# Two graph attention layers on 128 graphs: one rotation of four PSUM banks, both layer 1 sums in the odd slot, and the upper parts of k and lk ahead of the layer 1 norm rows on ScalarE

## The chip, the core and the metric

The kernel runs on one core of a Trainium2 chip. The metric is the device time of one execution in microseconds; below 2867.19 us (the median of three runs, 2866.46 to 2871.12) stands for the kernel before.

## What is computed

The input x holds 128 graphs of 128 nodes with 512 features each, adj their 128 x 128 boolean adjacency. Two layers follow one another, each with a residual sum:

```
h = max(layernorm(x), 0)
# layer 0, 8 heads of 64:
m = h @ map_w.T + map_b;  q, k = m @ q_w.T + q_b, m @ k_w.T + k_b
cos_adj = cosine(m_head_i, m_head_j) > 0.1          (masked)
p = softmax(where(mask, -1e10, q k^T / 8)) * keep
A = cos_adj * p;  x = x + relu((A @ (h @ gcn_map_w.T + b)) @ gcn_W.T / (rowsum(A) + 1))
# layer 1, 4 heads of 64:
h = max(layernorm(x), 0)
x = x + softmax(where(adj, (h Wq)(h Wk)^T / 8, -max)) @ (h Wv) @ Wo + bo
```

## The kernel before

All matrices are float32 in the reference and are held here as an upper and a lower float16 part. A product of two such takes three matmul passes (upper by upper, upper by lower, lower by upper). To split a tile, ScalarE copies it to float16 (a function named ..._upper), and GpSimd or VectorE subtracts that from the float32 tile (..._lower). Small per-node tiles are then turned by transposing DMAs that SP issues.

The work is a software pipeline written out by hand. A slot belongs to one graph, and in slot n each stage serves the graph of its own distance: projections of m are two graphs ahead, q and k one ahead, layer 0 scores serve graph n, layer 1 runs 3 to 5 behind. Even and odd slots have different work, since the projections treat two graphs at once (256 columns): the even slot has m, v and lv, the odd one q, k, lq and lk. Each of the five engines has its own function slot(s) that lists its stages in order, separately for even and odd, and over_slots writes all slots of all engines out one after another. There is no planner: an engine does its list in order, and semaphores hold it wherever a stage needs something of another engine. A stage at the head of an engine's list therefore holds back everything behind it in that list.

TensorE's list in the even slot: layer 0 scores, cosines, layer 1 scores (l1_scores), m in two halves, the weighted sums, output (wo), va, lv, vb, the layer 1 sums. In the odd slot: scores, cosines, q in two halves, weighted sums, layer 1 sums, norms, the first half of k, lq, the spreading of the inverse norms (bc0, bc1), the second half of k, output, lk.

A unit is what one of these stages writes into one PSUM bank of 512 floats. Before, there are two pairs of banks: proj_ps (13 units in a pair of slots) and mix_ps (7 units). Within each pair the banks alternate in the order of PROJ_UNITS and MIX_UNITS; start_proj and start_mix make TensorE wait until the unit two places back in the same pair has been read (proj_out, mix_out). proj_full and mix_full tell the readers that a unit is done.

The stages that matter at the boundary from odd to even slot, on ScalarE (L848 on): directions_upper twice, h1_rows (waits for ln1_step, that is GpSimd's norm_l1), qk_upper for the second half of k, h1_upper, lqk_upper for lk. On VectorE: k_lower (L966) for that half, result (L1084), lqk_lower (L991) for lk, and then the next slot's scores_mask. On GpSimd in the odd slot: ..., q_lower, e_lower (L588), directions_lower twice (L650), norm_l1 (L659 to L664), o1_lower (L577). TensorE's scores at the head of the even slot (L1313, s_ps) wait for k_lo, q_lo and x1_done; l1_scores waits for lk's lower part. In the trace both halves of q and k are called qk_sb (float32) and qk_hl (parts), and all of matmul helper row_pairs stands at L1313, features at L1295, rows at L1303.

Of the kernel before, what the change touches and what calls it, by code (L numbers as in the profile page):

```python
# [39 lines left out]
P = 128  # L40
# [40 lines left out]
class Slot:  # L81
# [20 lines left out]
    def _unit(self, units, name, back):  # L102
        def index(t):
            n = 0
            for u in range(FIRST_SLOT, t):
                n += sum(0 <= u + ahead < self.graphs for _, ahead in units[u % 2])
            for what, ahead in units[t % 2]:
                if what == name:
                    return n
                n += 0 <= t + ahead < self.graphs  # L110
            raise KeyError(name)

        at = Slot(self.n - back, self.i, self.graphs)
        return Unit(index(at.n) % 2, at.at(lambda t: index(t) // 2), at.at(lambda t: index(t) + 1))

    def proj(self, name, back=0):
        return self._unit(PROJ_UNITS, name, back)

    def mix(self, name, back=0):
        return self._unit(MIX_UNITS, name, back)  # L120

# [33 lines left out]
def build(nc, x, adj, map_w, map_b, q_w, q_b, k_w, k_b, gcn_map_w, gcn_map_b, gcn_W, Wq, Wk, Wv, Wo, bo, out):  # L155
# [13 lines left out]
    with ExitStack() as ctx:  # L169
# [115 lines left out]
        proj_ps = ctx.enter_context(nc.psum_tensor("proj_ps", [P, 2, 4 * P], F32))  # L285
        mix_ps = ctx.enter_context(nc.psum_tensor("mix_ps", [P, 2, 4 * P], F32))
# [32 lines left out]
        proj_full = sem("proj_full")  # L319
        proj_out = [sem(f"proj_out{i}") for i in range(2)]  # L320
        mix_full = sem("mix_full")
        mix_out = [sem(f"mix_out{i}") for i in range(2)]
# [70 lines left out]
        def prep_bank(u):  # L393
            return (proj_ps, mix_ps)[u % 4 // 2][:, u % 2]
# [18 lines left out]
        def _(sp):  # L413
# [17 lines left out]
            def turn_o1(s):  # L431
                if s.has(-5):
                    sp.wait_ge(o1_lo, s.at(lambda t: t - 5 + 1))
                    settle(sp, settled_sp, s.i)
                    if s.has(-6):
                        sp.wait_ge(proj_full, s.proj("wo", back=1).full)
# [4 lines left out]
            def turn_h1(s):  # L441
                if s.has(-2):
# [3 lines left out]
                    if s.has(-4 - back):  # L446
                        sp.wait_ge(proj_full, s.proj("lv", back=back).full)
# [4 lines left out]
            def turn_p1(s, behind):  # L452
                if s.has(-behind):
                    sp.wait_ge(p1_lo, s.at(lambda t: t - behind + 1))
                    settle(sp, settled_sp, s.i)
                    if s.has(-behind - 2):
                        sp.wait_ge(mix_full, s.mix("o1", back=behind - 2).full)
# [27 lines left out]
            def store(s):  # L485
                if s.has(-5):
                    u = s.proj("wo")
                    sp.wait_ge(proj_out[u.bank], u.before + 1)
                    settle(sp, settled_sp, s.i)
                    sp.dma_start(out[s.graph(-5)], ybuf[:, s.n % 2, :]).then_inc(y_out, 16)  # L490

            def turn_x(s):
                for a in range(2):
                    if s.has(3 + a):
                        sp.wait_ge(h_lo, s.at(lambda t: t + 3 + a + 1))
                        settle(sp, settled_sp, s.i)
                        if s.has(-1):
                            sp.wait_ge(proj_full, s.proj("k23", back=2).full)
# [40 lines left out]
        def _(pool):  # L539
# [72 lines left out]
            def keep_and_block(s):  # L612
# [7 lines left out]
                if s.has(0):  # L620
                    if s.has(-4):
                        u = s.mix("s1b", back=1) if s.odd else s.mix("s1a")
                        pool.wait_ge(mix_out[u.bank], u.before + 1)
# [9 lines left out]
            def inverse_norms(s):  # L633
                if s.has(1):
                    u = s.mix("norm")
                    pool.wait_ge(mix_out[u.bank], u.before + 1)
                    nc.gpsimd.tensor_tensor(inv_norm[:, :], sq_sum[:, :], minus_half[:, :], ALU.pow).then_inc(inv_norm_done, 1)  # L637
                    if s.has(-1):
                        pool.wait_ge(mix_full, s.mix("bc1", back=2).full)
# [85 lines left out]
        def _(act):  # L725
# [35 lines left out]
            def v_upper(s, name, ahead):  # L761
                if s.has(ahead):
                    u = s.proj(name)
                    act.wait_ge(proj_out[u.bank], u.before + 1)
# [5 lines left out]
            def lv_upper(s):  # L770
                if s.has(-4):
                    u = s.proj("lv")
                    act.wait_ge(proj_full, u.full)
                    if s.has(-5):
                        act.wait_ge(mix_full, s.mix("o1", back=1).full)
                    r = (s.n - 4) % 4
                    nc.scalar.activation(lv_sb[:, 0, r:r + 2, :, 0:DH],
                                         proj_ps[:, u.bank, :].rearrange("p (a h d) -> p a h d", a=2, h=H1),
# [29 lines left out]
            def o1_upper(s, behind):  # L808
                if s.has(-behind):
                    u = s.mix("o1", back=behind - 4)  # L810
                    act.wait_ge(mix_out[u.bank], u.before + 1)
# [3 lines left out]
            def qk_upper(s, name, src, dst, half, done):  # L815
                if s.has(1):
                    u = s.proj(f"{name}{2 * half}{2 * half + 1}")
                    act.wait_ge(proj_out[u.bank], u.before + 1)
# [4 lines left out]
            def squares(s):  # L823
                if s.has(2):
                    u = s.proj("m23")
                    act.wait_ge(proj_out[u.bank], u.before + 1)
                    if s.has(0):
                        act.wait_ge(mix_full, s.mix("norm", back=1).full)
                    nc.scalar.activation(sq_t[:, :, :], m_sb[:, :, :], ACT.Square).then_inc(squared, 1)

            def directions_upper(s, g):
                if s.has(1):
                    u = s.mix(f"bc{g}")
                    act.wait_ge(mix_out[u.bank], u.before + 1)
# [5 lines left out]
            def lqk_upper(s, name, dst, k):  # L840
                if s.has(-3):
                    u = s.proj(name)
                    act.wait_ge(proj_full, u.full)
                    if s.has(-5):
                        act.wait_ge(mix_full, s.mix("s1b", back=1).full)
                    nc.scalar.activation(dst[:, 0].rearrange("p c n -> p (c n)"), proj_ps[:, u.bank, :], ACT.Copy,
                                         scale=unscale[:, k:k + 1]).then_inc(lqk_hi, 1)

            def slot(s):
                if s.odd:  # L850
# [45 lines left out]
        def _(dve):  # L896
# [21 lines left out]
            def l1_mask(s, behind):  # L918
                if s.has(-behind):
                    b = (s.n - behind) % 2  # L920
                    u = s.mix("s1a" if behind == 4 else "s1b")
# [552 lines left out]
```

## Time and profile before

| what | value |
|---|---|
| median of three runs | 2867.19 us |
| the profiled execution | 2866.04 us, its span 2864.2 us |
| TensorE busy | 2635.6 us, 92% |
| VectorE, GpSimd, ScalarE busy | 70%, 70%, 59% |
| TensorE's mean granted clock | 0.972 |
| mean busy share of the DMA engines | 53.5% |

The span runs from the first to the last instruction of the execution that the profiler recorded; the rest of its time lies around it. Busy time of an engine is the union of its instructions' times. Matmuls overlap one another, so a busy TensorE need not be at its peak. "Idle before" an instruction is the time in which its engine did nothing just ahead of it, with the operation that ended the wait behind an arrow.

### The profile page before, as it was taken

The numbers are of one execution on the slowest core, as the hardware profiler recorded it, in microseconds if no ns is written. First come the engines' busy times: TensorE is split into PE (matmuls) and PEld (weight loads), VectorE is DVE, ScalarE is ACT, GpSimd is POOL, SyncE is SP. The second block draws the span as 40 slices with busy tenths as digits, with TensorE's granted clock in tenths as the row PEclk, the third lists the DMA queues.
The fourth block names the chain that finished last, engine by engine and source line by source line (L and its number), as shares of the span: only waits on it lengthen the run. The fifth ranks groups of instructions, "written<-read, shape, count | busy, mean of one in ns | idle before, by whom it ended". The sixth has DMA issues, their size and how long they took to land.

```text
span 2864.2 us, 78990 instructions
## 1 busy us (share of the span) xinstructions
PE 2635.6 (92%) x30809; PEld 2103.3 (73%) x30809; DVE 2011.8 (70%) x3457; ACT 1684.7 (59%) x4501; POOL 1993.1 (70%) x2332
## 2 busy tenths in 40 slices
PE   5789999999999999999999999999999999999985
PEld 3567777777777777777777777777777777777763
DVE  4367777777777777777777777777777777777763
ACT  1256666665666655666665566566556656656653
POOL 0377677677677677777877777787777778767762
PEclk7899999999999999999999999999999999999997
DMA  3145555655555555655655565565566555555543
GB/s 100 35 87 107 102 107 114 104 105 111 103 104 112 111 105 108 118 101 108 114 109 109 105 119 103 105 114 110 101 115 117 102 107 114 110 96 114 113 87 71
DMA packets 829123, 299.08 MB, mean 104 GB/s; under 512 B 772560, under 2 KB 778192, under 8 KB 828752
## 3 DMA queue, kind: packets, MB, share of 16 engines
q1 hardware_dynamic: 828752, 294.04, 53.5%
q8 instruction: 245, 4.01, 0.6%
q14 instruction: 126, 1.03, 0.1%
HBM read 75.80 MB, written 33.55 MB: 38 GB/s over the span
## 4 chain that ended last, share of the span: by engine, by line
PE 54%; POOL 24%; issue 8%; DVE 7%; ACT 3%; DMA 2%; SPq 1%; DVEq 0%; ACTq 0%; POOLq 0%
PE proj_ps L1295 23%; PE proj_ps L1303 18%; POOL inv_norm L637 6%; POOL e_ec L588 4%; POOL dir_hl L650 4%; PE s_ps L1313 4%; PE c_ps L1313 3%; POOL qk_hl L609 2%; POOL inv_rows L643 2%; DVE qk_hl L966 2%; PE mix_ps L1313 2%; ACT qk_hl L821 2%; DMA o_t<-o_hl 2%; PE s_ps L1354 1%; POOL rstd L662 1%
## 5 line engine op out<-in xcount | busy, mean ns | idle before, releaser
L732 ACT ACTIVATE e_ec<-e_ec,neg_mx 128x128 f32<-128x128 f32 x1024 | 396.0, 388 | 4.3
L966 DVE TENSOR_TENSOR qk_hl<-qk_sb,qk_hl 128x512 f16<-128x512 f32 x128 | 125.2, 978 | 355.0 <-ACT qk_hl L821 354.6
L583 POOL TENSOR_TENSOR p_hl<-p_sb,p_hl 128x512 f16<-128x512 f32 x128 | 148.3, 1159 | 314.8 <-ACT p_hl L753 314.8
L1295 PE MATMUL proj_ps<-h_t,w_m_hi 128*128 128x256 f16 x2048 | 350.7, 278 | 9.4 <-DMA h_t<-h_hl 9.4
L1295 PE MATMUL proj_ps<-h_t,w_k_hi 128*128 128x256 f16 x2048 | 344.6, 274 | 0.0
L1295 PE MATMUL proj_ps<-h_t,w_q_hi 128*128 128x256 f16 x2048 | 339.5, 273 | 0.0
L1303 PE MATMUL proj_ps<-w_v_hi,h_t 128*128 128x512 f16 x1024 | 325.4, 379 | 0.0
L588 POOL TENSOR_TENSOR e_ec<-e_ec 128x1024 f16<-128x1024 f32 x128 | 287.2, 2244 | 17.1 <-ACT e_ec L759 17.1
L1295 PE MATMUL proj_ps<-h_t,w_m_lo 128*128 128x256 f16 x1024 | 283.9, 277 | 0.0
L1295 PE MATMUL proj_ps<-h_t,w_k_lo 128*128 128x256 f16 x1024 | 280.1, 274 | 0.0
L1295 PE MATMUL proj_ps<-h_t,w_q_lo 128*128 128x256 f16 x1024 | 279.1, 273 | 0.0
L786 ACT ACTIVATE h_sb<-x,shift,rstd 128x512 f32<-128x512 f32 x128 | 103.4, 808 | 231.5 <-POOL shift L664 231.5
L1313 PE MATMUL s_ps<-qk_hl 64*128 64x128 f16 x3072 | 112.6, 222 | 130.3 <-DVE qk_hl L966 130.3
L1295 PEld LDWEIGHTS proj_ps<-h_t,w_m_hi 128*128 128x128 f16 x2048 | 198.8, 100 | 42.7 <-issue 12.2
L571 POOL TENSOR_TENSOR h_hl<-h_sb,h_hl 128x512 f16<-128x512 f32 x128 | 153.9, 1203 | 104.6 <-ACT h_hl L794 104.6
L1295 PEld LDWEIGHTS proj_ps<-h_t,w_q_hi 128*128 128x128 f16 x2048 | 195.2, 98 | 28.5
L1295 PEld LDWEIGHTS proj_ps<-h_t,w_k_hi 128*128 128x128 f16 x2048 | 196.4, 98 | 21.9
L637 POOL TENSOR_TENSOR inv_norm<-sq_sum,minus_half 128x16 f32<-128x16 f32 x64 | 186.5, 2913 | 26.3 <-DVE sq_sum L1025 26.3
L1313 PEld LDWEIGHTS s_ps<-qk_hl 64*128 64x128 f16 x3072 | 89.7, 97 | 152.2 <-DVE qk_hl L966 148.1
L943 DVE SCALAR_TENSOR_TENSOR qk_sb<-proj_ps,unscale,bias_q 128x512 f32<-128x512 f32 x128 | 96.2, 751 | 144.1 <-PE proj_ps L1295 143.9
L1303 PEld LDWEIGHTS proj_ps<-w_v_hi,h_t 128*128 128x128 f16 x1024 | 100.1, 98 | 128.9 <-DVE m_sb L943 20.2
L1303 PE MATMUL proj_ps<-w_v_lo,h_t 128*128 128x512 f16 x512 | 194.0, 379 | 0.0
(205 smaller groups left out, 7866.9 us busy)
## 6 DMA issues: line engine op xcount, KB each, us to landing
xa<-in_x_dram SPq DMA_DIRECT2D x128, 256.0 KB, 3.5
xres<-in_x_dram SPq DMA_DIRECT2D x128, 256.0 KB, 2.8
out_dram<-ybuf SPq DMA_DIRECT2D x128, 256.0 KB, 2.5
h_t<-h_hl SPq DMA_TRANSPOSE x256, 3.2
ec_t<-e_ec SPq DMA_TRANSPOSE x256, 3.2
adj_in<-in_adj_dram SPq DMA_DIRECT2D x128, 16.0 KB, 2.1
p_t<-p_hl SPq DMA_TRANSPOSE x128, 3.3
o_t<-o_hl SPq DMA_TRANSPOSE x128, 3.8
```

Source lines behind the costliest of these rows:

```text
L571: nc.gpsimd.tensor_tensor(h1_hl[:, a, 1, :], h1_sb[:, a, :], h1_hl[:, a, 0, :], ALU.subtract).then_inc(h1_lo, 1)
L583: nc.gpsimd.tensor_tensor(p1_hl[:, b, 1], p1_sb[:, b], p1_hl[:, b, 0], ALU.subtract).then_inc(p1_lo, 1)
L588: nc.gpsimd.tensor_tensor(e_hl[:, 1], e_sb[:, :, :], e_hl[:, 0], ALU.subtract).then_inc(e_lo, 1)
L637: nc.gpsimd.tensor_tensor(inv_norm[:, :], sq_sum[:, :], minus_half[:, :], ALU.pow).then_inc(inv_norm_done, 1)
L650: nc.gpsimd.tensor_tensor(dir_hl[:, 1, :, cols], m_sb[:, :, cols], dir_hl[:, 0, :, cols], ALU.subtract).then_inc(dir_lo, 1)
L732: ins = nc.scalar.activation(e[:, h, :], e[:, h, :], ACT.Exp, bias=neg[:, h:h + 1], scale=SCALE, accum_out=sums[:, h:h + 1])
L786: nc.scalar.activation(h1_sb[:, a, :], x1[:, (s.n - 1) % 8, :], ACT.Relu, bias=shift1[:, 0:1], scale=rstd1[:, 0:1]).then_inc(h1_done, 1)
L943: nc.vector.scalar_tensor_tensor(out=dst[:, c0:c0 + 2, :], in0=proj_ps[:, u.bank, :].rearrange("p (c n) -> p c n", c=2), scalar=factor, in ...
L966: nc.vector.tensor_tensor(k_hl[:, 1, c, :], k_sb[:, c, :], k_hl[:, 0, c, :], ALU.subtract).then_inc(k_lo, 1)
L1295: ins = nc.tensor.matmul(out, w[a][:, i, c * P:(c + 1) * P], h[:, :, b, i, :], start=n == 0, stop=n == len(passes) - 1)
L1303: ins = nc.tensor.matmul(ps, h[:, a, i, :], w[b][:, i, :], start=first and n == 0, stop=n == len(passes) - 1)
L1313: ins = nc.tensor.matmul(outs[half][c], st[r, a, c, cols], mv[r, b, c, cols], start=n == 0, stop=n == 2)
```

## The change

The two pairs of banks become one rotation of four: unit_ps with UNITS, 20 units in a pair of slots, so that a unit's bank is its place modulo 4, and start_unit waits for the unit four places back. All proj_full, mix_full, proj_out and mix_out waits of the five engines are put on unit_full and unit_out accordingly. The layer 1 scores take two neighbouring banks (s1a, s1b) at the start of the even slot; since both masks read both banks, output in the even slot waits for the second mask as well. The layer 1 sums of the even graph (now o1e) move from the end of the even slot to the odd one, behind the first half of q; VectorE's o1_rows for them goes behind q_features(s, 0). On ScalarE in the odd slot, the upper part of k's second half and that of lk go ahead of h1_rows. The diff, cut to its core:

```diff
-PROJ_UNITS = (
-    (("m01", 2), ("m23", 2), ("wo", -5), ("va", 2), ("lv", -4), ("vb", 3)),
-    (("q01", 1), ("q23", 1), ("k01", 1), ("lq", -3), ("k23", 1), ("wo", -5), ("lk", -3)),
+UNITS = (
+    (("s1a", -4), ("s1b", -4), ("m01", 2), ("m23", 2), ("wo", -5), ("va", 2), ("lv", -4), ("vb", 3)),
+    (("q01", 1), ("o1e", -5), ("q23", 1), ("o1o", -4), ("norm", 1), ("k01", 1), ("lq", -3), ("bc0", 1), ("bc1", 1), ("k23", 1), ("wo", -5),
+     ("lk", -3)),
 )
-MIX_UNITS = (
-    (("s1a", -4), ("s1b", -4), ("o1", -4)),
-    (("o1", -4), ("norm", 1), ("bc0", 1), ("bc1", 1)),
-)
+BANKS = 4
...
+    def unit(self, name, back=0):
+
+        t = self.n - back
+        place, used, full = 0, [0] * BANKS, 0
+        for u in range(FIRST_SLOT, t + 1):
+            for what, ahead in UNITS[u % 2]:
+                if u == t and what == name:
+                    return Unit(place % BANKS, used[place % BANKS], full + 1)
+                if 0 <= u + ahead < self.graphs:
+                    used[place % BANKS] += 1
+                    full += 1
+                place += 1
+        raise KeyError(name)
...
-        proj_ps = ctx.enter_context(nc.psum_tensor("proj_ps", [P, 2, 4 * P], F32))
-        mix_ps = ctx.enter_context(nc.psum_tensor("mix_ps", [P, 2, 4 * P], F32))
+        unit_ps = ctx.enter_context(nc.psum_tensor("unit_ps", [P, BANKS, 4 * P], F32))
...
@@ ScalarE, slot(s), odd @@
                     directions_upper(s, 0)
                     directions_upper(s, 1)
+                    qk_upper(s, "k", k_sb, k_hl, 1, k_hi)
+                    lqk_upper(s, "lk", lk_hl, LK)
                     h1_rows(s)
-                    qk_upper(s, "k", k_sb, k_hl, 1, k_hi)
                     h1_upper(s)
-                    lqk_upper(s, "lk", lk_hl, LK)
...
@@ VectorE, slot(s), odd @@
                 if s.odd:
+                    q_features(s, 0)
                     o1_rows(s, 5)
-                    q_features(s, 0)
                     q_features(s, 1)
...
@@ TensorE @@
+            def start_unit(s, name):
+
+                u = s.unit(name)
+                wait(pe, unit_out[u.bank], u.before)
+                return unit_ps[:, u.bank]
...
+            def l1_sums(s, behind):
+                if s.has(-behind):
+                    g = s.n - behind
+                    pe.wait_ge(p1_in[g % 2], s.at(lambda t: 16 * ((t - behind) // 2 + 1)))
+                    if behind == 5:
+                        u = s.unit("lv", back=1)
+                        pe.wait_ge(unit_out[u.bank], u.before + 1)
+                    ps = start_unit(s, "o1e" if behind == 5 else "o1o")
...
             def output(s):
                 if s.has(-5):
                     pe.wait_ge(o1_in, s.at(lambda t: 16 * (t - 5 + 1)))
-                    ps = start_proj(s, "wo")
+                    if not s.odd and s.has(-4):
+                        u = s.unit("s1b")
+                        pe.wait_ge(unit_out[u.bank], u.before + 1)
+                    ps = start_unit(s, "wo")
...
                 if s.odd:
                     qk_part(s, "q", w_q, 0)
+                    l1_sums(s, 5)
                     qk_part(s, "q", w_q, 1)
                     weighted_sums(s)
-                    l1_sums(s)
+                    l1_sums(s, 4)
                     norms(s)
...
                     l1_values(s)
                     v_part(s, "vb", 1)
-                    l1_sums(s)
```

## Rows read from the trace of the kernel before

**Rows 1.** Busy time of each engine over the span, from the page's first part.

```profile
PE 2635.6 (92%) x30809; PEld 2103.3 (73%) x30809; DVE 2011.8 (70%) x3457; ACT 1684.7 (59%) x4501; POOL 1993.1 (70%) x2332
```

**Rows 2.** TensorE's waits over the span: who waited for whom, us in total, times, longest.

```profile
PE s_ps L1313 <- DVE qk_hl L966: 130.3, 64, 4.2
...
PE proj_ps L1397 <- DVE lq_hl L991: 9.5, 9, 1.1
...
PE proj_ps L1295 <- DVE qk_sb L943: 1.6, 9, 0.2
```

**Rows 3.** Timeline of TensorE (start, duration, what, count, idle before) at an even slot's head.

```profile
1433.84 0.84 PE L1313 MATMUL s_ps<-qk_hl 64*128 64x128 f16 x24 [1.96 <-DVE qk_hl L966]
1434.52 1.05 PE L1313 MATMUL c_ps<-dir_hl 64*128 64x128 f16 x24
1435.36 1.49 PE L1313 MATMUL mix_ps<-lk_hl,lq_hl 64*128 64x128 f16 x24
```

**Rows 4.** Timeline of VectorE, the end of the odd slot before it.

```profile
1425.10 0.82 DVE L966 TENSOR_TENSOR qk_hl<-qk_sb,qk_hl 128x512 f16<-128x512 f32 x1 [1.79 <-ACT qk_hl L821]
...
1427.79 0.75 DVE L943 SCALAR_TENSOR_TENSOR qk_sb<-proj_ps,unscale,bias_k 128x512 f32<-128x512 f32 x1
1433.09 0.69 DVE L966 TENSOR_TENSOR qk_hl<-qk_sb,qk_hl 128x512 f16<-128x512 f32 x1 [4.55 <-ACT qk_hl L821]
```

**Rows 5.** Timeline of ScalarE in the same odd slot.

```profile
1417.32 0.40 ACT L813 ACTIVATE o_hl<-o_sb 128x256 f16<-128x256 f32 x1
...
1431.73 0.81 ACT L786 ACTIVATE h_sb<-x,shift,rstd 128x512 f32<-128x512 f32 x1 [3.29 <-POOL shift L664]
1432.45 0.61 ACT L821 ACTIVATE qk_hl<-qk_sb 128x512 f16<-128x512 f32 x1
```

**Rows 6.** Timeline of GpSimd, the same odd slot and the even one after it.

```profile
1425.33 2.58 POOL L588 TENSOR_TENSOR e_ec<-e_ec 128x1024 f16<-128x1024 f32 x1
1427.91 2.27 POOL L650 TENSOR_TENSOR dir_hl<-m_sb,dir_hl 128x512 f16<-128x512 f32 x2
...
1431.64 0.67 POOL L577 TENSOR_TENSOR o_hl<-o_sb,o_hl 128x256 f16<-128x256 f32 x1
...
1443.15 1.16 POOL L583 TENSOR_TENSOR p_hl<-p_sb,p_hl 128x512 f16<-128x512 f32 x1 [4.69 <-ACT p_hl L753]
```

**Rows 7.** Windows: stretch, length, each engine's busy time, granted clock, DMA share.

```profile
0.00:250.00 250.00, 190.41 (x1600) 144.10 (x1600) 125.91 (x210) 91.20 (x212) 110.92 (x143) 0.87 0.33 77
...
2774.00:2864.20 90.20, 52.10 (x529) 35.11 (x529) 38.25 (x71) 32.69 (x93) 26.27 (x35) 0.76 0.38 81
1351.08:1369.08 18.00, 18.00 (x211) 13.10 (x212) 16.19 (x28) 12.25 (x36) 11.74 (x17) 1.00 0.58 126
1433.84:1453.30 19.46, 19.46 (x211) 14.37 (x212) 16.19 (x28) 12.26 (x36) 11.38 (x17) 0.91 0.69 117
```

**Rows 8.** Timelines of VectorE and GpSimd where k's lower part meets e_ec's subtraction.

```profile
325.32 2.46 DVE L966 TENSOR_TENSOR qk_hl<-qk_sb,qk_hl 128x512 f16<-128x512 f32 x1 [2.23 <-ACT qk_hl L821]
...
325.10 2.13 POOL L588 TENSOR_TENSOR e_ec<-e_ec 128x1024 f16<-128x1024 f32 x1
```

**Rows 9.** Timelines of TensorE, ScalarE and VectorE at the end of an lv unit.

```profile
1407.41 0.38 PE L1303 MATMUL proj_ps<-w_v_hi,h_t 128*128 128x512 f16 x1
...
1407.62 0.69 ACT L777 ACTIVATE lv_sb<-proj_ps,v_scale 128x512 f16<-128x512 f32 x1 [0.80 <-PE proj_ps L1303]
...
1408.34 0.75 DVE L981 SCALAR_TENSOR_TENSOR lv_sb<-proj_ps,v_scale,lv_sb 128x512 f16<-128x512 f32 x1 [0.64 <-ACT lv_sb L777]
```

**Rows 10.** The core's span and mean granted clock.

```profile
core 0: 2864.2 us, clock 0.972
```

**Rows 11.** Timelines of VectorE and TensorE: second layer 1 mask and output, even slot.

```profile
1398.14 0.68 DVE L925 TENSOR_TENSOR p_sb<-mix_ps,block 128x512 f32<-128x512 f32 x1
...
1400.55 0.38 PE L1397 MATMUL proj_ps<-bias_y,three_rows 128*128 128x512 bf16 x1
```

**Rows 12.** The o_t transposes: time from issue to landing, minimum, median and maximum.

```profile
DMA to landing us min/median/max: 2.4/3.8/6.4
```

More of the change, by code:

```diff
@@ L435, in turn_o1 @@
                     if s.has(-6):
-                        sp.wait_ge(proj_full, s.proj("wo", back=1).full)
+                        sp.wait_ge(unit_full, s.unit("wo", back=1).full)
                     settle(sp, settled_sp, s.i)
@@ L446, in turn_h1 @@
                     if s.has(-4 - back):
-                        sp.wait_ge(proj_full, s.proj("lv", back=back).full)
+                        sp.wait_ge(unit_full, s.unit("lv", back=back).full)
                     settle(sp, settled_sp, s.i)
@@ L456, in turn_p1 @@
                     if s.has(-behind - 2):
-                        sp.wait_ge(mix_full, s.mix("o1", back=behind - 2).full)
+                        sp.wait_ge(unit_full, s.unit("o1e" if behind == 4 else "o1o", back=1).full)
                     settle(sp, settled_sp, s.i)
@@ L486, in store @@
                 if s.has(-5):
-                    u = s.proj("wo")
-                    sp.wait_ge(proj_out[u.bank], u.before + 1)
+                    u = s.unit("wo")
+                    sp.wait_ge(unit_out[u.bank], u.before + 1)
                     settle(sp, settled_sp, s.i)
@@ L497, in turn_x @@
                         if s.has(-1):
-                            sp.wait_ge(proj_full, s.proj("k23", back=2).full)
+                            sp.wait_ge(unit_full, s.unit("k23", back=2).full)
                         settle(sp, settled_sp, s.i)
@@ L621, in keep_and_block @@
                     if s.has(-4):
-                        u = s.mix("s1b", back=1) if s.odd else s.mix("s1a")
-                        pool.wait_ge(mix_out[u.bank], u.before + 1)
+                        u = s.unit("s1b", back=1) if s.odd else s.unit("s1a")
+                        pool.wait_ge(unit_out[u.bank], u.before + 1)
                     settle(pool, settled_pool, s.i)
@@ L634, in inverse_norms @@
                 if s.has(1):
-                    u = s.mix("norm")
-                    pool.wait_ge(mix_out[u.bank], u.before + 1)
+                    u = s.unit("norm")
+                    pool.wait_ge(unit_out[u.bank], u.before + 1)
                     nc.gpsimd.tensor_tensor(inv_norm[:, :], sq_sum[:, :], minus_half[:, :], ALU.pow).then_inc(inv_norm_done, 1)
                     if s.has(-1):
-                        pool.wait_ge(mix_full, s.mix("bc1", back=2).full)
+                        pool.wait_ge(unit_full, s.unit("bc1", back=2).full)
                     pool.wait_ge(inv_norm_done, s.at(lambda t: (t + 1) // 2 + 1))
@@ L809, in o1_upper @@
                 if s.has(-behind):
-                    u = s.mix("o1", back=behind - 4)
-                    act.wait_ge(mix_out[u.bank], u.before + 1)
+                    u = s.unit("o1e" if behind == 5 else "o1o")
+                    act.wait_ge(unit_out[u.bank], u.before + 1)
                     wait(act, o1_in, s.at(lambda t: 16 * (t - behind)))
@@ L816, in qk_upper @@
                 if s.has(1):
-                    u = s.proj(f"{name}{2 * half}{2 * half + 1}")
-                    act.wait_ge(proj_out[u.bank], u.before + 1)
+                    u = s.unit(f"{name}{2 * half}{2 * half + 1}")
+                    act.wait_ge(unit_out[u.bank], u.before + 1)
                     wait(act, s_full, s.at(lambda t: t + 1))
@@ L824, in squares @@
                 if s.has(2):
-                    u = s.proj("m23")
-                    act.wait_ge(proj_out[u.bank], u.before + 1)
+                    u = s.unit("m23")
+                    act.wait_ge(unit_out[u.bank], u.before + 1)
                     if s.has(0):
-                        act.wait_ge(mix_full, s.mix("norm", back=1).full)
+                        act.wait_ge(unit_full, s.unit("norm", back=1).full)
                     nc.scalar.activation(sq_t[:, :, :], m_sb[:, :, :], ACT.Square).then_inc(squared, 1)
@@ L832, in directions_upper @@
                 if s.has(1):
-                    u = s.mix(f"bc{g}")
-                    act.wait_ge(mix_out[u.bank], u.before + 1)
+                    u = s.unit(f"bc{g}")
+                    act.wait_ge(unit_out[u.bank], u.before + 1)
                     if g == 0:
@@ L920, in l1_mask @@
                     b = (s.n - behind) % 2
-                    u = s.mix("s1a" if behind == 4 else "s1b")
-                    dve.wait_ge(mix_full, s.mix("s1b").full)
+                    u = s.unit("s1a" if behind == 4 else "s1b")
+                    dve.wait_ge(unit_full, s.unit("s1b").full)
+                    pair = s.unit("s1a").bank
                     dve.wait_ge(blocked1, s.at(lambda t: t - behind + 1))
@@ L933, in l1_max @@
                     b = (s.n - behind) % 2
-                    u = s.mix("s1a" if behind == 4 else "s1b")
-                    dve.wait_ge(mix_out[u.bank], u.before + 1)
+                    u = s.unit("s1a" if behind == 4 else "s1b")
+                    dve.wait_ge(unit_out[u.bank], u.before + 1)
                     wait(dve, neg_lmx_done, s.at(lambda t: t - behind - 1))
```

164 lines of the change are left out of this document (64 added, 100 removed).

## Prediction

> **What bounds the kernel now.** I read the busy shares first. TensorE is busy for 92% of the span and no other engine for more than 70% [rows 1], so a change can help only where it fills TensorE's idle time or shortens its matmuls. Next come TensorE's waits over the span [rows 2]. The reader is to see one large line that recurs: the scores matmul waits for VectorE's lower part (of k, as the timeline shows), 130.3 us in 64 waits, once a pair of slots. Two others recur and are small: 9.5 us in 9 waits of the output matmuls for the lower part of lq, and 1.6 us in 9.
>
> Then the timelines around one such wait. TensorE starts the scores at 1433.84 after 1.96 us of idle time, so lk's last matmul ended at 1431.88 [rows 3]. VectorE wrote k's second half in f32 at 1427.79 to 1428.54, but took its lower part only at 1433.09 [rows 4], because ScalarE made the upper part at 1432.45 [rows 5]. ScalarE had been idle for 3.29 us, since 1428.44: next in its order stood the layer 1 norm rows (h_sb), and these waited for the shift from GpSimd until 1431.73 [rows 5], because GpSimd reaches it only after e_ec and both subtractions of dir_hl [rows 6]. So k, ready at 1428.5, stood behind norm rows that nothing needed soon. The bound at this place is ScalarE's order, fed by GpSimd's chain.
>
> Last the windows. An even slot (scores to scores) takes 18.00 us at a granted clock of 1.00, and 19.46 at 0.91 where the clock fell after the wait [rows 7]: there the scores start at full speed, but the cosines (1.05) and layer 1 scores are slow [rows 3], down to the 1.2 GHz level.
>
> **Part 1: k's second upper part and lk's upper part ahead of h1_rows on ScalarE.** k's upper part can start when k in f32 is ready, 1428.6, and ends 0.61 later at 1429.2. VectorE is idle then (it stood idle 4.55 us before 1433.09 [rows 4]) and asks for the lower part at about 1429.2. It meets GpSimd's second dir_hl subtraction, 1429.0 to 1430.18 [rows 6]. What such a meeting costs is seen elsewhere: a lower part of k that began 0.22 after a GpSimd subtraction took 2.46 us and ended 0.55 after that one's end, against 0.69 alone [rows 4, 8]. So I put the end at 1430.18 + 0.6 = 1430.8. From both sides: 1429.9 if they do not disturb each other, 1433.0 if GpSimd went on through its o_hl subtraction (1431.64 + 0.67 = 1432.31 [rows 6]) without letting VectorE in. I take 1430.8, by the nearest row. It is 1.1 before 1431.88, so the port delay is hidden by lk's matmuls and the 1.96 wait goes whole.
>
> The Trainium skill, SBUF — State Buffer, section "SBUF: two separate sides", says that VectorE with two SBUF inputs and GpSimd share a port pair under an exclusive lock, held for the whole instruction by whichever came first. It speaks against this move, as k's lower part now falls beside GpSimd work. The 2.46 us row agrees with it. By the rule the sum stays as it is, because the lock is free again at 1430.18; without the rule it would be the same.
>
> What is late next: lk. Its matmuls end at 1431.88, the scores follow (0.68 to the next start [rows 3]) and the cosines, with as many matmuls of the same shape, so layer 1 scores could start 1.36 later. They need lk's lower part. The same pattern stands at lv [rows 9]: next matmul 1407.41, ScalarE starts 1407.62 (+0.21), VectorE starts 1408.34 (+0.93) and ends at +1.68; TensorE starts 0.06 after such an end [rows 3, 4]. So layer 1 scores start at +1.74: a new wait of 0.38 a pair, 64 pairs, 24.3 us. Bounds: nothing if ScalarE starts sooner, 0.75 more if VectorE were still at the result, an operation of the same size. Output's matmuls come ahead of lk's, so the result can follow k's lower part at once and is done by 1430.8 + 0.75 = 1431.6: I keep 0.38.
>
> The norm rows now come behind lk's upper part: h1_rows 1432.8 to 1433.5, h1_upper to 1434.2, instead of 1433.58. GpSimd's subtraction on it moves back by the same 0.6 us. Behind it on GpSimd stand v's lower parts and the two small mask operations, and then 4.69 us of idle time before p_hl [rows 6], which covers it; the transposed rows are read only a slot later. No DMA is issued by a moved step here. SP's store of the result gets free earlier, since the result no longer stands behind the late lower part of k.
>
> **Part 2: the clock.** The fall comes in some of the pairs, after the wait. Its count: lost clock over the span is (1 − 0.972) × 2864 = 80 us; the first 250 us hold 0.13 × 250 = 32.5 and the last 90 hold 0.24 × 90 = 21.6, so 26 are left for the steady part; one fall is 0.09 × 19.46 = 1.75, which makes 15 falls, and each costs 19.46 − 18.00 = 1.46 us: 22 us [rows 7, 10]. I take all of it as regained: the fall read here came 1.5 us after a wait of 1.96 [rows 3], most waits of that length bring none, and only 0.38 us of idle time is left. Bounds: 0 to 22 regained, and if the 0.38 wait made it fall in every pair, 71 lost.
>
> **Part 3: one rotation of four banks.** A unit now waits for the one four places back instead of two places back in its own pair. Going through all 20 places of a pair, the unit four back has left its bank before its successor starts, mostly by several us. Output keeps its wait for lq (it is again four back), lk no longer waits for k23: −1.6 us [rows 2]. One wait is new: in the even slot output waits for both layer 1 masks. The second mask ends at 1398.82 and output starts at 1400.55 [rows 11]: cover 1.7. VectorE ended lk's lower part some 1.2 to 1.4 after the scores' start (two operations of 0.75 behind 1433.78) and will end it 1.68 after; TensorE is itself 0.38 later. So at least 1.6 is left. Cost nothing; if the cover were gone, 1 us late is 64 us. Behind the waiting output stand va, lv and vb.
>
> **Part 4: the layer 1 sums of the even graph** go from the end of the even slot to behind the first half of q. Its 12 matmuls are the same 0.47 us, so the sum is zero. Its rows on VectorE now come behind q's first half; o1_upper on ScalarE runs only after the eight exponentials, which fill ScalarE to 1417.3 in that slot (no idle time before its row [rows 5]), so nothing behind it moves. The scores of the odd slot start 0.47 earlier and meet the same ScalarE. Semaphore waits added and removed balance. Bounds: −3 to +5 us.
>
> **The sum**, against the profiled execution (span 2864.2, time 2866.04, so 1.84 around it): 2864.2 − 130.3 + 24.3 − 22 − 1.6 = 2734.6; with 1.84 it is 2736.4. The median of the runs, 2867.19, stands 1.15 above the profiled one: 2737.5. The longest of the 64 waits (4.2 us) and two more lie in the ramp, where another wait may take over: up to +10.
>
> **Rivals.** A, the clock falls stay: for it, they need not come from the wait; against it, every slot that shows one began with a wait. 22 more: 2760.
>
> B, the late pairs become the rule. In 9 pairs k's first lower part asks just after GpSimd took the port [rows 8], instead of 1425.33 − 1425.10 = 0.23 us before [rows 4, 6], because ScalarE's second o_hl, ahead of it, waits for the o_t transpose. Output then waits up to 1.1 for lq's lower part [rows 2]; with the slower start of what follows I estimate 1.4 a pair. For it: landing times run from 2.4 to 6.4 us [rows 12], and the same traffic goes through in a span 4% shorter. Against it: everything from the slot's start to that issue is unchanged. 63 − 9 = 54 more × 1.4 = 76: 2814.
>
> C, GpSimd keeps VectorE out until 1432.31: scores at 1433.0, layer 1 scores at 1434.5 (result and lk's lower part queue behind), 0.86 gained instead of 1.58. 64 × 0.72 = 46 and half of the falls, 11: 2795.
>
> D, slower: the o_t transpose, on SP behind the h transposes and x loads, lands so late that k's first lower part begins after GpSimd's e_ec subtraction has ended, 1425.33 + 2.13 − 1425.10 = 2.36 us later than in the normal pair [rows 4, 6, 8]; from there each us costs a us. Loss 1.4 × 63 − 13 = 75 by then; to eat the gain of 130 takes 55 / 63 = 0.87 more, so it decides at 3.2 us later on average. At 4 us later: 63 × 3.04 − 13 = 179: 2916. Against it, the latest landing seen is only 2.6 above the median.
>
> E, the wait has another releaser behind it (q's lower part, x1) and nothing moves: 2867. Against it, q's lower part stands ahead of e_ec on GpSimd and so ended by 1425.33 [rows 6], and x1 stands ahead of k's first lower part on VectorE, so before 1425.10 [rows 4].
>
> **How the numbers follow.** Forecast 0.79, A 0.05, B 0.06, C 0.05, D 0.03, E 0.02. The likeliest gives 2737.5; its own range, from late pairs between 0 and 25, some falls, and the ramp, is 2718 to 2765. To reach 8 in 10 with A and the nearer parts of C: 2716 to 2780. Faster by over 0.2% (about what a measurement can tell here) is all but D and E: 0.95; within 0.2%: 0.02; slower: 0.03.
>
> **What would show it.** The wait of s_ps for qk_hl shrinks from 130 us to a few; a new wait of layer 1 scores for lk_hl of about 0.38 us, 64 times; k's second lower part takes 1.3 to 1.7 us instead of 0.69; the clock over the steady part is 1.00; the even slot, which loses the layer 1 sums (0.47) and gains the wait, goes from 18.00 to 17.9; no wait of output for a mask. Wrong, if output waits for p_sb in the even slot, if the waits for lq_hl are many more than 9, or if half-speed stretches stay without a wait before them.

## The result and the profile after

The changed kernel takes 2720.55 us (median of four runs, 2716.03 to 2724.04) against 2866.82 for the kernel before, run beside it: a ratio of 0.9486, 95% interval 0.9469 to 0.9504. The profiled execution took 2716.03 us, its span is 2714.2. It is the quickest of the four, 4.5 below the median, while the profiled run of before lay 1.15 below the 2867.19 of its three. One execution of a later experiment, the kernel with o1_upper later, took 15177.52 us, unexplained, and the ratio given there is that of the other five.

First the waits. The ramp is the first 250 us or so, in which the pipeline fills, and the drain the last 90; between them lies the steady part. The list of TensorE's waits over the span, which answers to [rows 2], with total us, times and the longest:

```profile
PE unit_ps L1383 <- DVE lq_hl L981: 12.8, 11, 1.7
...
PE unit_ps L1383 <- DVE p_sb L915: 5.7, 3, 2.2
...
PE s_ps L1298 <- DVE qk_hl L956: 4.6, 2, 2.3
PE unit_ps L1298 <- DVE lk_hl L981: 3.1, 2, 1.6
```

The 130.3 us of the scores matmul are down to 4.6, both in the ramp. The expected new wait of the layer 1 scores for lk's lower part does not show here as 64 entries, because the modelled end of the cosines, 1394.90 in the rows below, covers half of it and leaves 0.13 of idle time; the two entries that stand there lie in the drain, and were there before. It shows in the list of the weight loads, which stand ahead of the matmuls, between 250 and 2630 us:

```profile
PEld unit_ps L1298 <- DVE lk_hl L981: 17.5, 60, 0.3
```

The three waits of output for the second layer 1 mask (p_sb) are new, and all lie behind 2620 us, in the drain. They did not lengthen it: from 2733.06 on it took 131.14 us before, and from 2582.54 on it takes 131.66 now.

Next the head of an even slot on TensorE, which answers to [rows 3]:

```profile
1393.39 0.84 PE L1298 MATMUL s_ps<-qk_hl 64*128 64x128 f16 x24
1394.07 0.83 PE L1298 MATMUL c_ps<-dir_hl 64*128 64x128 f16 x24
1395.03 0.84 PE L1298 MATMUL unit_ps<-lk_hl,lq_hl 64*128 64x128 f16 x24
```

The scores have no idle time before them and the cosines run at full speed. Where scores to cosines take 0.68, cosines to layer 1 scores take 0.96: 0.28 of it is the wait for lk.

The timelines of ScalarE, VectorE and GpSimd at the end of the odd slot ahead of it, which answer to [rows 4 to 6], tell the new order:

```profile
1390.15 0.63 ACT L810 ACTIVATE qk_hl<-qk_sb 128x512 f16<-128x512 f32 x1
1393.50 0.69 ACT L835 ACTIVATE lk_hl<-unit_ps,unscale 128x512 f16<-128x512 f32 x1 [2.71 <-PE unit_ps L1280]
1394.08 0.80 ACT L775 ACTIVATE h_sb<-x,shift,rstd 128x512 f32<-128x512 f32 x1
```

```profile
1389.37 0.75 DVE L933 SCALAR_TENSOR_TENSOR qk_sb<-unit_ps,unscale,bias_k 128x512 f32<-128x512 f32 x1
1390.81 1.50 DVE L956 TENSOR_TENSOR qk_hl<-qk_sb,qk_hl 128x512 f16<-128x512 f32 x1 [0.70 <-ACT qk_hl L810]
1392.23 0.74 DVE L1074 SCALAR_TENSOR_TENSOR ybuf<-unit_ps,y_scale,x 128x512 f32<-128x512 f32 x1
1394.22 0.75 DVE L981 SCALAR_TENSOR_TENSOR lk_hl<-unit_ps,unscale,lk_hl 128x512 f16<-128x512 f32 x1 [1.25 <-ACT lk_hl L835]
```

```profile
1389.49 2.27 POOL L639 TENSOR_TENSOR dir_hl<-m_sb,dir_hl 128x512 f16<-128x512 f32 x2
1391.85 0.51 POOL L648 TENSOR_SCALAR ve<-mv 128x1 f32<-128x1 f32 x1
```

k's upper part now starts 0.03 after k itself is there. Its lower part takes 1.50 us instead of 0.69: it asks 0.20 after the start of GpSimd's second dir_hl subtraction (1390.61, the second of the two instructions in the first row) and ends at 1392.31, 0.55 after that one's end (1391.76) and 1.08 before TensorE needs it. lk's way is: next matmul of TensorE 1393.39, ScalarE +0.11, VectorE +0.83, end +1.58, layer 1 scores +1.64.

Last the windows, which answer to [rows 7]; the second row is one even slot:

```profile
250.00:2630.00 2380.00, 2361.66 (x28643) 1897.26 (x28640) 1898.19 (x3176) 1573.39 (x4195) 1875.62 (x2154) 1.00 0.60 115
1393.39:1411.18 17.79, 17.67 (x200) 12.73 (x200) 15.32 (x26) 13.96 (x38) 12.22 (x18) 1.00 0.61 121
```

The granted clock is 1.00 over the whole steady part: not one fall to the 1.2 GHz level is left there. TensorE is busy for 99% of it.

Each window of the next two rows holds the same 59 pairs of slots, and they show where the time went; first the kernel before, from the first even slot behind the ramp on, then the changed one:

```profile
250.88:2733.06 2482.18, 2353.48 (x28203) 1892.37 (x28204) 1818.19 (x3128) 1536.49 (x4131) 1828.83 (x2125) 0.99 0.57 108
```

```profile
241.62:2582.54 2340.92, 2325.37 (x28204) 1869.59 (x28204) 1870.46 (x3128) 1550.11 (x4130) 1849.28 (x2128) 1.00 0.60 115
```

141.3 us went here; most of the other 8.7 went in the ramp (134.08 to 250.88 before, 132.53 to 241.62 after: 7.7). A normal pair went from 41.38 us (18.00 and 23.38) to 39.51 (17.79 and 21.72), 1.87 less, 110 in 59 pairs. The 16 clock falls are gone, 23. The late pairs are those of rival B, in which k's first lower part comes behind the start of e_ec's subtraction. Their odd slot took 25.46 before, 2.08 more than normal, and takes 22.93 now, 1.21 more, and they are 8 instead of 9: 9. The sum is 142.

### The profile page after: what moved, and what is told of

Same layout as the page of the kernel before. It is cut to its first block, busy times and chain, and to the rows that moved or that the text cites. A ratio compares the mean times of both kernels' runs of the same rounds, so it can differ in the third digit from the quotient of the medians.

```text
span 2714.2 us, 78928 instructions
## 1 busy us (share of the span) xinstructions
PE 2603.4 (96%) x30809; PEld 2075.9 (76%) x30809; DVE 2066.0 (76%) x3457; ACT 1699.2 (63%) x4501; POOL 2013.7 (74%) x2332
## 4 chain that ended last, share of the span: by engine, by line
PE 82%; DVE 5%; ACT 3%; POOL 3%; DMA 3%; issue 2%; SPq 1%; ACTq 0%; DVEq 0%; POOLq 0%
PE unit_ps L1280 45%; PE unit_ps L1288 22%; PE s_ps L1338 3%; PE unit_ps L1298 2%; PE unit_ps L1357 2%; DVE lk_hl L981 2%; DMA o_t<-o_hl 2%; PE s_ps L1298 2%; ACT lk_hl L835 2%; PE unit_ps L1372 1%; PE c_ps L1298 1%; PE unit_ps L1348 1%; PE unit_ps L1383 1%; DVE qk_hl L956 1%; POOL h_hl L591 1%
## 5 line engine op out<-in xcount | busy, mean ns | idle before, releaser
L1280 PE MATMUL unit_ps<-h_t,w_m_hi 128*128 128x256 f16 x2048 | 343.0, 275 | 9.4 <-DMA h_t<-h_hl 9.4
L1280 PE MATMUL unit_ps<-h_t,w_k_hi 128*128 128x256 f16 x2048 | 344.7, 274 | 0.0
L1280 PE MATMUL unit_ps<-h_t,w_q_hi 128*128 128x256 f16 x2048 | 342.8, 273 | 0.0
L1288 PE MATMUL unit_ps<-w_v_hi,h_t 128*128 128x512 f16 x1024 | 325.0, 379 | 0.0
L1280 PE MATMUL unit_ps<-h_t,w_m_lo 128*128 128x256 f16 x1024 | 280.7, 274 | 0.0
L1280 PE MATMUL unit_ps<-h_t,w_k_lo 128*128 128x256 f16 x1024 | 280.2, 274 | 0.0
L1280 PE MATMUL unit_ps<-h_t,w_q_lo 128*128 128x256 f16 x1024 | 279.1, 273 | 0.0
L1280 PEld LDWEIGHTS unit_ps<-h_t,w_m_hi 128*128 128x128 f16 x2048 | 196.3, 98 | 39.2 <-issue 9.8
L1280 PEld LDWEIGHTS unit_ps<-h_t,w_k_hi 128*128 128x128 f16 x2048 | 196.4, 98 | 22.1
L1288 PE MATMUL unit_ps<-w_v_lo,h_t 128*128 128x512 f16 x512 | 194.0, 379 | 0.0
```

Of the source, the lines that this page charges most:

```text
L1280: ins = nc.tensor.matmul(out, w[a][:, i, c * P:(c + 1) * P], h[:, :, b, i, :], start=n == 0, stop=n == len(passes) - 1)
L1288: ins = nc.tensor.matmul(ps, h[:, a, i, :], w[b][:, i, :], start=first and n == 0, stop=n == len(passes) - 1)
```

## The experiments

Each kernel ran beside the kernel before on one chip. The kernel before gave medians of 2855 to 2864 on these chips, and single times from 2843 to 2874, so ratios stand beside the times.

**The order alone.** To the kernel before, only this (and nothing of banks or sums):

```diff
                     directions_upper(s, 1)
+                    qk_upper(s, "k", k_sb, k_hl, 1, k_hi)
+                    lqk_upper(s, "lk", lk_hl, LK)
                     h1_rows(s)
-                    qk_upper(s, "k", k_sb, k_hl, 1, k_hi)
                     h1_upper(s)
-                    lqk_upper(s, "lk", lk_hl, LK)
```

> The kernel before with one edit: on ScalarE in the odd slot the upper parts of k's second half and of lk go ahead of h1_rows. Banks and layer 1 sums as before. Theory (the order carries the gain, the four banks only a small remainder): the 1.96 us waits and the clock falls of the steady part go, a wait of layer 1 scores for lk's lower part of about 0.28 us a pair comes, as in the changed kernel, and the small waits of va's weight loads (some 0.13 us a pair, 8 us in all) stay: about 2720 + 8 + 2 = 2730 us. Rival (the rotation of four banks is what lets the scores start early, the order alone runs into a bank that is not free): above 2790 us, with a new TensorE wait for a bank in the odd slot.

Measured: 2724.48 us, ratio 0.9538 (0.9518 to 0.9559). The order carries nearly the whole gain (the changed kernel, on the same chip, has 0.9506 below); the rival is out. The weight loads between 250 and 2590 us show what the old banks still cost:

```profile
PEld proj_ps L1303 <- DVE m_sb L943: 28.1, 59, 0.5
PEld mix_ps L1313 <- DVE lk_hl L991: 16.9, 58, 0.3
PEld proj_ps L1303 <- DVE ybuf L1084: 15.8, 59, 0.3
```

va waits for the bank that VectorE frees with m's second half, in every pair, and the layer 1 values (lv) behind it for the result's bank.

**The banks and the sums alone.** The changed kernel with the ScalarE lines above put back as they were.

> The changed kernel with ScalarE's old order in the odd slot (h1_rows, k's second upper part, h1_upper, lk's upper part); four banks and moved layer 1 sums stay. Theory: the wait of the scores for k's lower part is back at about 1.96 us a pair, 64 times, and so are some 15 falls of the clock in the steady part; only the 0.13 us a pair at va and 1.6 us at lk are gained: about 2867 - 10 = 2857 us. Rival on the clock (the falls came from something in the old bank order or the place of the layer 1 sums, not from the wait): the wait is back but the granted clock of the steady part is 1.00, about 2834 us.

Measured: 2853.37 us beside 2857.50, ratio 0.9993 (0.9975 to 1.0012): less than the 10 us expected, and within what the runs can tell from nothing. A normal pair does get shorter, from 41.39 to 41.24 us (medians of the two traces), which would be 10 us in 64; why the medians of the runs show only 4 stays open. The wait is back, 131.4 us in 64, and the falls with it. They are 9 in the 59 pairs of the profiled run, where 16 stood before and 15 were expected; that run is the quickest of ten, 2840.64 us. One of the nine:

```profile
963.07 0.84 PE L1298 MATMUL s_ps<-qk_hl 64*128 64x128 f16 x24 [1.96 <-DVE qk_hl L956]
963.75 1.07 PE L1298 MATMUL c_ps<-dir_hl 64*128 64x128 f16 x24
964.61 1.49 PE L1298 MATMUL unit_ps<-lk_hl,lq_hl 64*128 64x128 f16 x24
...
963.07:982.17 19.10, 19.05 (x198) 13.84 (x201) 15.83 (x27) 12.27 (x36) 11.04 (x17) 0.91 0.68 119
```

The first three rows are TensorE's timeline, the last the window of that slot: 19.10 us at 0.91, where a slot without a fall takes 17.50. So the falls follow the wait and not the bank order.

**Only k ahead, lk behind.** In the changed kernel h1_rows and h1_upper go between the two upper parts:

```diff
                     qk_upper(s, "k", k_sb, k_hl, 1, k_hi)
-                    lqk_upper(s, "lk", lk_hl, LK)
                     h1_rows(s)
                     h1_upper(s)
+                    lqk_upper(s, "lk", lk_hl, LK)
```

> The changed kernel with lk's upper part behind h1_rows and h1_upper again; only k's second upper part stays ahead. Theory: the scores start without a wait, but lk's upper part now waits behind the norm rows, whose shift comes about 0.2 us after lk's matmuls end; two ScalarE operations of 0.8 and 0.6 us then stand ahead of it, so layer 1 scores start about 1.5 us later a pair than in the changed kernel: 64 x 1.5 = 96, about 2817 us, with a TensorE wait of unit_ps for lk_hl of some 1.6 us, 64 times; and if the clock falls after such waits, some more (up to 20 us). Rival (lk's place does not matter, its wait is hidden behind scores and cosines): 2720 to 2730 us.

Measured: 2817.93 us, ratio 0.9872 (0.9834 to 0.9909), as expected to 1 us, which is closer than the four runs (2807.71 to 2833.05) can tell. TensorE's waits and one even slot:

```profile
PE unit_ps L1298 <- DVE lk_hl L981: 108.1, 64, 2.7
...
1406.13:1425.43 19.30, 17.62 (x199) 12.75 (x199) 15.31 (x26) 13.96 (x38) 12.24 (x18) 1.00 0.66 108
```

Moving k alone gives about a quarter of the gain (1.3% of 5%): lk is next on the path at once. Most waits are 1.6 us here, and of the 59 in the steady part only two are followed by a fall of the clock, both of 2.49 us.

**The result ahead of k's second lower part on VectorE.**

```diff
                     k_features(s, 1)
-                    k_lower(s, 1)
                     result(s)
+                    k_lower(s, 1)
                     lqk_lower(s, "lk", lk_hl, LK, 1)
```

> The changed kernel with VectorE's result(s) ahead of k's second lower part in the odd slot. Theory (k's lower part waits for GpSimd's dir_hl subtraction to end, 1.50 us instead of 0.69): k's lower part starts about 0.8 us later, runs 0.7 to 0.85 us, and ends at the same distance from the end of the subtraction, so the time stays within 3 us of the changed kernel's 2720. Rival (its 1.50 us are its own slowness beside other traffic and not a wait): it takes 1.5 us again, ends 0.8 us later, at about the end of lk's matmuls, and the result of the slot no longer hides anything: 2720 to 2730 us with small waits of s_ps for qk_hl.

Measured: 2716.78 us, ratio 0.9513 (0.9496 to 0.9529), the changed kernel's time within its spread. VectorE's and GpSimd's rows:

```profile
1394.53 0.70 DVE L956 TENSOR_TENSOR qk_hl<-qk_sb,qk_hl 128x512 f16<-128x512 f32 x1
...
1392.41 2.27 POOL L639 TENSOR_TENSOR dir_hl<-m_sb,dir_hl 128x512 f16<-128x512 f32 x2
```

Asked 0.15 us before dir_hl's end (1394.68), k's lower part takes 0.70 and ends 0.55 behind that end, the same distance as when it asks earlier. 0.70 is what it takes alone, so this row shows no wait by itself; beside the 1.50 us of the changed kernel it shows that the 1.50 are a wait for GpSimd's running instruction and not slowness of its own.

**The changed kernel again**, beside the next three.

> The changed kernel itself, to stand beside the three edits of it on the same chip: 2714 to 2724 us, with 5 to 12 late pairs (an odd slot of 22.9 us instead of 21.7) and no fall of the clock in the steady part.

Measured: 2716.00 us, ratio 0.9506 (0.9484 to 0.9528), with 5 waits of output for lq_hl in the steady part.

**o1_upper later on ScalarE.**

```diff
                     e_upper(s)
-                    o1_upper(s, 4)
                     qk_upper(s, "k", k_sb, k_hl, 0, k_hi)
                     lqk_upper(s, "lq", lq_hl, LQ)
+                    o1_upper(s, 4)
```

> The changed kernel with ScalarE's second o1_upper in the odd slot behind the upper parts of k's first half and of lq. Theory (a late pair comes from the landing of the o_t transpose, through this o1_upper, which holds back k's upper part until GpSimd has taken the port for e_ec): k's first lower part no longer depends on the landing, no odd slot takes 22.9 us, no TensorE wait for lq_hl in the steady part: 8 x 1.2 = 10 us less, about 2711 us. Rival (the late pairs come from GpSimd or from k's features, not from the landing): they stay at about 8, 2720 us.

Measured: 2724.86 us, ratio 0.9534 (0.9511 to 0.9556): slower than the changed kernel by 9. The late pairs went as the theory said, and the forecast of the time failed: 14 us above it, and slower instead of quicker. No wait for lq_hl is left and no odd slot is late, but every odd slot takes 21.99 instead of 21.72. The weight loads' waits, then VectorE and GpSimd:

```profile
PEld unit_ps L1357 <- POOL inv_rows L632: 17.1, 58, 0.3
...
1385.97 1.00 DVE L956 TENSOR_TENSOR qk_hl<-qk_sb,qk_hl 128x512 f16<-128x512 f32 x1
...
1385.82 1.63 POOL L632 COPY inv_rows<-inv_norm 128x512 f32<-128x512 f32 x2
```

k's first lower part now asks 0.15 after the start of the first of GpSimd's two inv_rows copies, gets in between them, and these end 0.46 later (1.63 for 1.17), which TensorE feels as 0.28. One odd slot of the changed kernel's 59 takes 21.99 too, by the same meeting (asked 0.15 after the first copy's start, 1.00 us), there because o_t landed early.

**lk ahead of output** on TensorE and in the units' order, and its lower part ahead of the result on VectorE:

```diff
-    ... ("k23", 1), ("wo", -5),
-     ("lk", -3)),
+    ... ("k23", 1), ("lk", -3),
+     ("wo", -5)),
...
                     k_lower(s, 1)
-                    result(s)
                     lqk_lower(s, "lk", lk_hl, LK, 1)
+                    result(s)
...
-                    output(s)
                     lqk_part(s, "lk", w_lk)
+                    output(s)
```

> The changed kernel with lk ahead of output in the odd slot, on TensorE and in the units' order, and lk's lower part ahead of the result on VectorE. Theory (the last wait of a normal pair is lk's way over ScalarE and VectorE, 0.28 us before the layer 1 scores): lk's matmuls end 1.5 us earlier, the wait goes, the even slot takes 17.5 instead of 17.79 us: 64 x 0.28 = 18 less, about 2702 us; late pairs stay, now with lk waiting for lq's lower part. Rival (the gap between cosines and layer 1 scores is something of TensorE's own, at the change to tiles of 64 rows, and not lk's lower part): the even slot stays at 17.79, 2720 us.

Measured: 2696.63 us, ratio 0.9439 (0.9416 to 0.9463), 19 below the changed kernel beside it. The window of an even slot:

```profile
1346.78:1364.28 17.50, 17.50 (x201) 12.72 (x201) 15.49 (x27) 13.39 (x37) 12.46 (x18) 1.00 0.70 122
```

17.50 instead of 17.79: the 0.28 us were lk's way, and the rival is out. The late pairs stay, 8 of 59.

**Both edits.**

> Both edits, o1_upper later and lk ahead of output. Theory: both gains, since they lie in different slots: 2720 - 10 - 18, about 2692 us, with no TensorE wait left in the steady part. Rival (one gain is given back, as lk's start now falls into what the landing used to cover): no better than the better one alone, 2702 us.

Measured: 2703.01 us, ratio 0.9460 (0.9438 to 0.9482), even slots 17.50, odd slots 21.99, no late pair. Neither case as written, though the rival's 2702 us is near: lk's gain came whole, and what o1_upper's move costs in every odd slot stayed.

**The second layer 1 mask behind the gate.**

```diff
                     m_features(s, 0)
-                    l1_mask(s, 3)
                     gate(s)
+                    l1_mask(s, 3)
```

> The changed kernel with VectorE's second layer 1 mask behind the gate in the even slot. Theory (output in the even slot now waits for this mask, and has 1.7 us of cover): the mask ends some 2.7 us later, at about 0.95 us after output could start, so TensorE waits about 0.95 us for p_sb in every pair, 64 x 0.95 = 61: about 2778 us. Rival (the mask is not on the path, output is held by something else): 2716 us.

Measured: 2782.82 us, ratio 0.9717 (0.9679 to 0.9755). VectorE and TensorE:

```profile
1397.91 0.68 DVE L915 TENSOR_TENSOR p_sb<-unit_ps,block 128x512 f32<-128x512 f32 x1
...
1398.69 0.38 PE L1383 MATMUL unit_ps<-bias_y,three_rows 128*128 128x512 bf16 x1 [0.89 <-issue]
```

Output starts 0.10 after the mask's end (1397.91 + 0.68; the profile itself names no releaser), and the even slot takes 18.84, 1.05 more (0.95 expected). The new wait of part 3 is real, and in the changed kernel it is hidden: there the mask ends 1.72 to 1.73 ahead of output in every even slot of the steady part, as much as [rows 11] have.

**k's first lower part behind the inv_rows copies**, on top of both edits:

```diff
                 if s.has(1):
+                    if half == 0:
+                        dve.wait_ge(inv_rows_done, s.at(lambda t: t + 1 + 2))
                     dve.wait_ge(k_hi, s.at(lambda t: t + 1 + half + 1))
```

> As with both edits (second o1_upper later, lk ahead of output), and VectorE's k_lower(s, 0) also waits for GpSimd's second inv_rows copy. Theory (moving o1_upper took the late pairs away, but let k's first lower part meet the inv_rows copies, which then ended 0.28 us later than TensorE's spreading needs them; put behind the copies it meets q's subtraction instead, which nobody waits for soon): no late pair, odd slot 21.7 us, even slot 17.5 us, no TensorE wait in the steady part: about 2688 us, the least of all. Rival (k's lower part pushes q's and so e_ec's and dir_hl's subtraction back, and k's second lower part with them): odd slot 22 us or more, 2700 us or more.

Measured: 2687.60 us, ratio 0.9391 (0.9365 to 0.9416), the quickest of all. VectorE and GpSimd, and an even slot:

```profile
1371.15 1.63 DVE L958 TENSOR_TENSOR qk_hl<-qk_sb,qk_hl 128x512 f16<-128x512 f32 x1 [0.97 <-POOL inv_rows L632]
...
1369.94 1.17 POOL L632 COPY inv_rows<-inv_norm 128x512 f32<-128x512 f32 x2
1371.08 1.16 POOL L598 TENSOR_TENSOR qk_hl<-qk_sb,qk_hl 128x512 f16<-128x512 f32 x1
...
1339.47:1356.97 17.50, 17.50 (x200) 12.73 (x199) 15.49 (x27) 13.40 (x37) 12.46 (x18) 1.00 0.68 121
```

The copies take 1.17 again and odd slots 21.71 to 21.72. The lower part asks 0.07 after GpSimd began q's subtraction, and ends 0.54 after its end. It does so in all 64 pairs. It costs VectorE 1.63 us and TensorE nothing. An added wait made the kernel faster by moving a collision to where nobody waits.

**The layer 1 sums of the even graph back at the even slot's end**, in the rotation of four banks (the edit cut to its core):

```diff
-    ... ("lv", -4), ("vb", 3)),
-    (("q01", 1), ("o1e", -5), ("q23", 1), ...
+    ... ("lv", -4), ("vb", 3), ("o1e", -4)),
+    (("q01", 1), ("q23", 1), ...
...
-                    l1_sums(s, 5)
...
                     v_part(s, "vb", 1)
+                    l1_sums(s, 4)
```

> The changed kernel with the layer 1 sums of the even graph back at the end of the even slot, in the rotation of four banks; ScalarE's new order stays. Theory (the place of the sums costs nothing, its readers stand behind ScalarE's exponentials either way): the even slot gets 0.37 us longer and the odd one 0.37 shorter, the time stays at 2716 within 4 us. Rival (their place is what gains beyond the order, since the scores of the odd slot start earlier): 2725 us or more.

Measured: 2719.33 us, ratio 0.9500 (0.9467 to 0.9533), even slots 18.16 and odd 21.35: 0.37 over and 0.37 under. The place of the sums is worth nothing, within 3 us. Against "the order alone", which differs in the banks, the even slot is 18.16 instead of 18.32: the rotation is worth 0.16 a pair, 10 us in 64.

## Why the prediction was right, and by how much it missed

The forecast was 2737.5 us, the result is 2720.55: the gain was 146 us where 130 were forecast. Against the profiled executions, 2736.4 was forecast and 2716.03 came, 20.4 less. The result lies in the range of 2716 to 2780, but near its lower end, since nearly all misses go the same way.

Part 1, k: right in mechanism and sizes. The 1.96 us wait went whole, the lower part met dir_hl's subtraction, took 1.50 (1.3 to 1.7 was said), and ended 1.08 before lk's matmuls did (1.1 was said). The rule of the Trainium skill, SBUF — State Buffer, section "SBUF: two separate sides", that the engine which comes first holds the shared port for its whole instruction, is borne out here: of the 111 lower parts of k in the changed kernel that asked while a GpSimd subtraction or copy was running and took over 0.76 us, 109 ended 0.53 to 0.56 after the end of that instruction, however early they had asked. The prediction left out a second consequence of this: whom a meeting delays depends on where it falls, as the o1_upper experiment showed.

Part 1, lk: right in kind, too large. The term was 0.38 a pair and measured 0.28, since ScalarE started 0.11 after TensorE's next matmul and not 0.21 as at lv [rows 9]. That is 64 × 0.10 = 6 us.

Part 2, the clock: right. 22 us were taken and 16 falls of 1.46, 23 us, went. The falls came back with the wait in the kernel that has only the banks. That so short a wait as lk's would bring none was a guess when it was made (its bounds ran to 71 us lost); the kernel with the late mask, in which 59 steady waits of 0.9 us brought none, bears it out.

Part 3: its waits were read right where TensorE's matmuls showed them, and one was missed. va and lv waited for their banks in the old pair, but through their weight loads, and the prediction read only the waits of the matmuls. The matmul list of before has nothing there, the weight loads' list of before, 250 to 2774 us, has it (va behind m_sb, lv behind ybuf):

```profile
PEld proj_ps L1303 <- DVE m_sb L943: 20.2, 44, 0.5
PEld proj_ps L1303 <- DVE ybuf L1084: 11.9, 44, 0.3
```

The term "lk no longer waits for k23, 1.6 us" should have been the whole worth of the rotation, 10 us. This is the mis-sized step that weighs most. The cover of the mask was right in the steady part: at least 1.6 us was said, and it is 1.73. In the drain it was not there three times (5.7 us), which cost nothing in the sum, as the drain kept its length.

Part 4: right, zero. The sums themselves are 0.37 us and not 0.47, by the two places of the last experiment; as they only move, the sum does not feel it, but the even slot, forecast at 17.9, is 17.79 by lk's 0.28 and the 0.13 to 0.16 of the banks.

lk and the banks explain 6 + 8 = 14 of the 20. Of the rest, some 4 lie in the removed wait itself: from lk's first matmul to the scores it was 4.74 us before (1429.10 to 1433.84) and is 2.71 now (1390.68 to 1393.39), 2.03 less where the idle time reads 1.96. The late pairs gave 9, of which the terms held 6: 9 times the 0.52 us by which their scores waited longer than others, and the 1.6. Ramp and drain gave 9 where the terms held about 11. That the runs of the changed kernel spread by 8 us, and the profiled one is at their low end, goes the other way in the median, which is 17 below the forecast.

Of the rivals, B showed itself to be a real mechanism, in 4 to 11 of the 59 steady pairs of every profiled run with the old place of o1_upper, and not the rule. That o_t's landing brings it about is shown by the kernel with o1_upper later and the two kernels built on it, in which none is left, and by the changed kernel's own trace: the second o1_upper, which a landing released each time, started 14.26 to 15.7 us after the slot's start in the 8 late odd slots and by 14.24 in the 51 others. A, C, D and E did not come.

## What to carry to other kernels

An in-order engine's list is worth reading for what stands behind a stage that waits: here two small copies behind norm rows that nobody needed soon held the bounding engine for 2 us in each of 64 pairs, and moving them gave 5%. Price the next operation on the same path as well (lk here), because moving the first alone gave a quarter. Read the waits of the weight loads beside those of the matmuls: banks that came free too late showed only there.

## What the runs showed of the hardware that was not expected

Two engines that share a port can be tuned by adding a wait: k's first lower part, put behind the copies on purpose, took 1.63 us instead of 1.00, and the kernel went from a ratio of 0.9460 to one of 0.9391 (2703.01 and 2687.60 us).

The clock's falls are no fixed price of a wait. In the steady part of the kernel before, none of 7 waits of 1.6 us was followed by one, 10 of 43 of 1.9 to 2.0 us, and 6 of 9 of 2.48 us; in the kernel with only the banks, 7 of 54 of 1.9 to 2.0 us and 2 of 4 of 2.8; in the kernel with lk behind, none of 54 up to 1.7 us and 2 of 5 of 2.49; in the kernel with the late mask, none of 59 of 0.9; after the 0.28 us of the changed kernel, none. So in these runs the chance rises with the wait's length, and no steady wait of 1.7 us or less was followed by a fall. The waits of different kernels stand at different places, and what picks the waits of one length was not tried and stays open.
